# Attention scores in float32r parts on half the array's rows, with the operand stacks copied head by head inside SBUF

## The reference

```
attn = softmax(einsum('bgdi,bgdj->bgij', q, k) * 16**-0.5)     # 2 x 8 heads, each 1024 x 1024
x = x + proj(Wp, bp, einsum('bgij,bgdj->bgdi', attn, v))
```

## Time and profile before

| | us |
|---|---|
| median of 3 runs | 368.35 (367.45 to 369.86) |
| the profiled execution | 367.55 |
| its span, first to last instruction | 365.6 |
| PE busy | 309.8 (85%) |
| DVE busy | 258.9 (71%) |
| ACT busy | 194.1 (53%) |
| POOL busy | 103.9 (28%) |
| mean granted PE clock | 0.925 |

### The profile page before, as it was taken

How to read it: one execution, slowest core, us unless ns; L and a number is a source line. 1 busy time by engine, 2 the same in 40 slices (tenths; PEclk the granted TensorE clock), 3 DMA queues, 4 the chain that set the end, 5 groups by cost and what they waited for, 6 DMA issues and landing times.

```text
span 365.6 us, 5601 instructions
## 1 busy us (share of the span) xinstructions
PE 309.8 (85%) x2046; PEld 106.8 (29%) x2046; DVE 258.9 (71%) x270; ACT 194.1 (53%) x359; POOL 103.9 (28%) x137
## 2 busy tenths in 40 slices
PE   7568779999990599999989999998981999698796
PEld 2244123333320133333323333333220344222242
DVE  3746759898970177887748988879898146999820
ACT  1406347767760267767757666766760546453132
POOL 5000051111010011011000036999980100894410
PEclk9969699999995599999999999999995799969899
DMA  5168950000699300000000000590000001960001
GB/s 198 29 210 129 162 104 3 30 31 0 125 120 125 37 1 2 1 2 3 1 2 0 2 2 3 158 204 5 1 2 0 0 0 74 192 167 2 0 0 57
DMA packets 11022, 19.97 MB, mean 55 GB/s; under 512 B 2035, under 2 KB 2931, under 8 KB 10995
## 3 DMA queue, kind: packets, MB, share of 16 engines
q1 hardware_dynamic: 10998, 19.64, 26.6%
HBM read 13.61 MB, written 5.54 MB: 52 GB/s over the span
## 4 chain that ended last, share of the span: by engine, by line
PE 59%; DVE 20%; DMA 9%; issue 4%; SPq 3%; ACT 2%; POOL 2%; DVEq 0%; ACTq 0%; POOLq 0%
PE ps L971 15%; PE ps L930 15%; PE ps L960 12%; DVE qs L744 11%; DMA qs<-mrows 6%; PE ps L1122 4%; DVE mx L696 4%; DMA ks<-parts_dram 2%; PE ps L1136 2%; SPq L331 2%; PE ps L951 2%; PE ps L1081 2%; PE ps L876 2%; PE ps L902 1%; ACT pr L568 1%
## 5 line engine op out<-in xcount | busy, mean ns | idle before, releaser
L696 DVE TENSOR_REDUCE mx<-ps 128x1 f32<-128x1024 f32 x128 | 154.3, 1221 | 55.5 <-PE ps L930 51.0
L568 ACT ACTIVATE pr<-ps 128x512 f32<-128x512 f32 x256 | 139.0, 595 | 98.8 <-PE ps L960 98.7
L960 PE MATMUL ps<-qs,ks 99*128 99x512 bf16 x256 | 79.6, 389 | 17.8 <-DMA qs<-mrows 16.9
L930 PE MATMUL ps<-ks,qs 96*128 96x512 bf16 x256 | 79.4, 395 | 10.7 <-DMA ks<-part 5.5
L971 PE MATMUL ps<-pr,va 128*32 128x256 f32 x1024 | 83.5, 398 | 0.0
L744 DVE SCALAR_TENSOR_TENSOR qs<-xpad,w,qs 128x512 f32<-128x512 f32 (+1 forms) x35 | 54.7, 1562 | 1.0
L433 POOL TENSOR_TENSOR mparts<-zeros,mx 128x8 bf16<-128x8 f32 x16 | 3.7, 230 | 169.0 <-DVE mx L696 169.0
L960 PEld LDWEIGHTS ps<-qs,ks 99*128 99x128 bf16 x256 | 24.5, 99 | 61.2 <-DMA qs<-mrows 16.7
L971 PEld LDWEIGHTS ps<-pr,va 128*32 128x32 f32 x1024 | 20.3, 109 | 51.4 <-issue 46.8
L930 PEld LDWEIGHTS ps<-ks,qs 96*128 96x128 bf16 x256 | 17.0, 99 | 55.5 <-issue 44.2
L1056 PE MATMUL ps<-xr,wt 128*32 128x512 f32 x224 | 30.0, 664 | 3.5 <-DMA xr<-pad_dram 3.5
(11 more groups left out here) (99 smaller groups left out, 229.2 us busy)
## 6 DMA issues: line engine op xcount, KB each, us to landing
parts_dram<-part SPq DMA_DIRECT2D x12, 256.0 KB, 2.6
xr<-pad_dram SPq DMA_DIRECT2D x8, 361.0 KB, 6.2
qs<-parts_dram SPq DMA_DIRECT2D x6, 256.0 KB, 11.6
ks<-parts_dram SPq DMA_DIRECT2D x6, 256.0 KB, 15.8
xr<-pad_dram SPq DMA_DIRECT2D x4, 304.0 KB, 10.7
qs<-parts_dram SPq DMA_DIRECT2D x6, 192.0 KB, 4.9
ks<-parts_dram SPq DMA_DIRECT2D x6, 192.0 KB, 7.3
xr<-pad_dram SPq DMA_DIRECT2D x4, 285.0 KB, 10.3
```

The lines of the kernel that those rows point to most:

```text
L568: nc.scalar.activation(pr[:, j % PR, c * HALF:(c + 1) * HALF], st[c], ACT.Exp, scale=SCALE).then_inc(exp_done, 1)
L696: nc.vector.tensor_reduce(mx[:, r, i:i + 1], sm[i % 2], AX.X, ALU.max).then_inc(max_done, 1)
L930: last = nc.tensor.matmul(sm[i % 2][:, c * HALF:(c + 1) * HALF], qs[0:STACK, bass.ds(s * N + i * P, P)], ks[0:STACK, bass.ds(s * N + c * H ...
L960: nc.tensor.matmul(st[c], ks[0:ROWS, bass.ds(t * N + j * P, P)], qs[0:ROWS, bass.ds(t * N + c * HALF, HALF)], start=True, stop=True).then_ ...
```

## The change

Queries and keys become two float32r parts (`PARTS = 2`), three products of parts in 3 x 16 = 48 rows, and 50 rows with the maxima (now positive, against rows of -1 in `ks`). A stack lies in partitions 0 to 49 or 64 to 113 (`rows_of`), and `qs` and `ks` shrink to four slots: two groups of rows by two cells of columns (`cell_of`). Head t uses the slot of head t - 4. The plan runs almost two heads ahead (`LAG = 1`, 15 tiles first), so that tile and transposed scores mostly belong to different groups of rows, and PE's order in a step alternates a half of `scores_t` (one step further ahead than before) and a half of `scores`. The stacks are copied from `hl` inside SBUF, six DMAs a head: for heads 0 and 1 the queries by SP and the keys by ACT's queue, for the others all by SP. POOL's `split_max` has two operations in place of five. The convolution's sums move to `hl` of image 1, so DVE's and POOL's taps wait for the stack of head 15. `replicate(0)` comes after `row_max(12)`.

```
-PARTS = 3                                   +PARTS = 2
-STACK = 6 * D                               +TERMS = 3; STACK = TERMS * D; GROUP_ROWS = 64; CELLS = 2
-LAG = 3                                     +LAG = 1; GAP = 3
+def max_turn(t): return 3 if t <= FINISH else 6 if t == FINISH + 1 else 5
+def u_turn(t): return 5 if t <= FINISH else 3
+def rows_of(t): return t // 2 % 2 * GROUP_ROWS
+def cell_of(t): return t % 2 * N
+        def stack(queue, i, t, n):
+            order, dst = ((Q_ORDER, qs), (K_ORDER, ks))[i]
+            queue.wait_ge(S(f"part{i}{n}", t // HEADS), 1)
+            h = t % HEADS
+            for g in range(TERMS):
+                if order[g] == n:
+                    queue.dma_start(
+                        dst[rows_of(t) + g * D:rows_of(t) + (g + 1) * D, cell_of(t):cell_of(t) + N].bitcast(F32),
+                        hl[h * D:(h + 1) * D, t // HEADS, i, n, :].bitcast(F32)).then_inc(S("stack", t), 16)
...
+            def next_stack(t):
+                sp.wait_ge(st_ready, 2 * NT * (t - 3))
+                for n in range(PARTS):
+                    stack(sp, 0, t, n)
+                    stack(sp, 1, t, n)
...
+            row_max(0)
+            for t in range(1, T):
+                if t + 3 < T:
+                    next_stack(t + 3)
+                row_max(t)
+                if t == FINISH + 3:
+                    replicate(0)
...
+            def scores_t(n, c):
+                t, j = divmod(n, NT)
+                if n:
+                    t_.wait_ge(exp_done, 2 * n + c - 1)
+                if j == 0 and c == 0:
+                    t_.wait_ge(s_mrow[t % 2], 16 * (t // 2 + 1))
+                rows = slice(rows_of(t), rows_of(t) + ROWS)
+                nc.tensor.matmul(st[c], ks[rows, ...], qs[rows, ...], start=True, stop=True).then_inc(st_ready, 1)
...
+            (head t, step j of PE; n = 8t + j)
+                    if n + 1 < NT * T:
+                        scores_t(n + 1, 0)
+                    if here:
+                        scores(*here[0], 1)
+                    if n:
+                        times_v(n - 1)
+                    if n + 1 < NT * T:
+                        scores_t(n + 1, 1)
+                    if j == max_turn(t) and t + 1 < T:
+                        turn_max(t + 1)
+                    if j == u_turn(t) and t:
+                        turn_u(t - 1)
...
+                    if then:
+                        scores(*then[0], 0)
```

More of the change, by code:

```diff
@@ L28 @@
 BF16 = mybir.dt.bfloat16
+F32R = mybir.dt.float32r
 ACT = mybir.ActivationFunctionType
@@ L531, in _ @@
                 a.wait_ge(S(f"proj{i}", 0), 1)
[L532 to L535, removed]
+                nc.scalar.activation(hl[:, 0, i, 0, :], sm[i], ACT.Identity, bias=vec(V_BQ + i))\
+                    .then_inc(S(f"part{i}0", 0), 1)
+            for n in range(PARTS):
+                for t in range(2):
+                    stack(nc.scalar, 1, t, n)
             values(0)
@@ L556, in copy_u, with head @@
+            def copy_u(t):
                 a.wait_ge(pv_done, NT * t + NT)
-                if later(t, 2):
+                if t >= 2:
                     a.wait_ge(ot_ready, t - 1)
-                nc.scalar.activation(u[:, r, :], pv[:, 0:2 * P], ACT.Copy).then_inc(u_ready, 1)
-            def head(t, r, turn=LAG + 2, also={}):
+                nc.scalar.activation(u[:, t % 2, :], pv[:, 0:2 * P], ACT.Copy).then_inc(u_ready, 1)
+            def head(t, also={}):
                 for j in range(NT):
+                    n = NT * t + j
@@ L579, in copy_oc @@
                 nc.scalar.activation(oc[:, 0, :], sm[0], ACT.Copy).then_inc(S("oc", 0), 1)
-            copy_max(0, 0)
-            head(0, 0)
-            head(1, 1)
-            with a.Fori(1, FINISH // 2) as pair:
-                head(2 * pair, 0)
-                head(2 * pair + 1, 1)
-            for t in range(FINISH - 1, T - 2):
-                head(t, t % 2, turned(t), also={LAG: copy_oc} if t == FINISH else {})
+            copy_max(0)
+            for t in range(T - 2):
+                head(t, {LAG + 1: copy_oc} if t == FINISH else {})
             def ln_square(k):
@@ L682, in _ @@
             v.wait_ge(S("w_soon"), 16)
-            split_rest(0)
+            low_part(0)
             gn_vareps(v, 1)
-            split_rest(1)
-            for i in range(2):
-                split_low(0, i)
+            low_part(1)
             gn_apply(v, 1, xs[:, 1, :], xn[:, 1, :], S("xn", 1))
@@ L951, in turn_u @@
                     last = nc.tensor.transpose(mi[:, OT_AT + i * P:OT_AT + (i + 1) * P],
[L952 removed]
+                                               u[:, t % 2, i * P:(i + 1) * P], ident)
                 last.then_inc(ot_ready, 1)
[L955 to L962 removed]
@@ L1036, in _ @@
                     t_.wait_ge(S("copied1"), 1)
-                    turn_max(0, 0)
-            t_.wait_ge(S("kones"), 16)
+                    turn_max(0)
+            t_.wait_ge(S("kones"), 32)
             t_.wait_ge(S("va", 1), 1)
+            for c in range(2):
+                scores_t(0, c)
+            scores(*plan[0][0][0], 0)
             also = {FINISH: [(LAG, finish_turn), (LAG + 2, finish_project)],
```

422 lines of the change are left out of this document (177 added, 245 removed).

## The result

The changed kernel takes 548.63 us (median of four runs, 540.85 to 552.13), the kernel before in the same job 369.11 (367.45 to 370.97): ratio 1.473, 95% interval 1.454 to 1.493. The direction was predicted; the size was not: 409, in a range of 382 to 452. The profiled execution took 547.0 us, span 545.2, mean granted clock 0.640 where it was 0.925.

The account below looks back on a forecast made before the run. PE's own order bound a plain head (12.6 us), DVE after head 13. Head 0 ends at 53.3, twelve waits add 69.6, heads 1 to 11 129.8; first tap 40.6 us later, span 406.2, forecast 409 us, range 382 to 452.

Parts of the forecast that it names:

- The order of SP's queue: Maxima's DMA behind next_stack's wait and six copies on SP: PE empty 5.8 us, twelve times, 69.6 in all.
- Rivals 2 and 3: SP's queue: 2, wait only 1.9 us, 342 us, chance 0.07; 3, wait 4.6, no clock lost, 374 us, 0.07.
- Side by side, in one pass: PE's score and transposed-score halves: float32r in one pass, two row groups at once, 0.22 us a pair instead of 0.44.
- Rival 1: PE's score pairs not side by side, or float32r taking twice the passes: 40 us more, 449 us; chance 0.20.
- The clock: After each PE wait, 4.7 us at half clock: 1.7 us lost, twelve times and once at the start; ends 0 and 2.1.
- 10.1 us a head: Plain head bound by DVE: eight maxima of 1.15 us, a division of 0.56, 0.3 for imperfect order; instead of 12.6.
- Head 0's transposed scores: Start of head 0 on PE: predicted at 41.5 us, before 41.98, with stacks landing about 1.6 us earlier.
- The tail: From DVE's first convolution tap to the span's end: kept at 117.2 us.
- The replicas: Head 12: replicate(0) before row_max(13) holds the maxima's DMA 14.5 us; a head covers all but 2.7.

Follow-up runs that it names:

- the filled kernels: changed_64 and side_by_side_64, whose score matmuls take in zero rows up to 62 and 64; 488.12 and 399.53 us.
- changed_64: The changed kernel, SP's order and waits kept, with score matmuls filled with zero rows to 62 and 64; 488.12 us, ratio 1.323.
- one_row_group_128: The changed kernel with row_max(t) before next_stack(t + 3), all stacks in one row group, zero rows to 126 and 128; 397.74 us, ratio 1.077.
- before_with_waits: The kernel before, with the wait of next_stack and eight 64 KB copies ahead of row_max(1) to row_max(12); 462.18 us, ratio 1.252.
- side_by_side_64: The changed kernel with row_max(t) before next_stack(t + 3) and zero rows to 62 and 64, pairs side by side; 399.53 us, ratio 1.08.
- copy_max_later: side_by_side_64 with ACT's copy of the turned maxima moved one step back in heads 0 to 9; 388.63 us, ratio 1.045.
- before_48_rows: The kernel before with two bf16 parts and three products, so 48 and 51 rows instead of 96 and 99; 487.48 us.

## Why the prediction was right in sign and wrong in size

**The order of SP's queue: right.** Predicted twelve waits of 5.8 us, 69.6 in all; the trace has 69.4. Issues 3.72 (3.9), landing 2.11 (2.0). Rivals 2 and 3 are out. What decided was six issues in a row: one alone, 0.62, is under a third of that landing, so what the prediction set side by side, six issues and one landing, says nothing on single DMAs. With the lost clock it is 7.4 a head where I had 7.5, by the filled kernels. That nearness is partly luck: 70.3 us of waits leave 1.5 a head for the clock (I had 1.7), but in changed_64 the clock was away for 3.6 to 21.4 us after a wait and not for 4.7, and it slowed heads of 13.45 us, not of 10.1.

**Side by side, in one pass: right.** Both kinds start at 177.09 together. The Trainium skill, TensorEngine Tiling (Array Packing), § Tiling Modes, says that different tiles can work in parallel; the trace agrees. For a half's 0.22 us stands one_row_group_128, where at 2.4 GHz the halves follow each other and start 0.23 and 0.24 apart (151.00 and 151.23, 152.69 and 152.93). Rival 1 is out; the range's upper end of 452 came from it and so from the wrong doubt. One thing was missed: the prediction took all pairs as side by side, and those at every second head's change are not.

**The clock: wrong, and the largest error.** The step was "with 4.7 us at half clock ... 1.7 us, twelve times". I took the 4.7 from a kernel whose score matmuls drive 96 and 99 rows. With 48 and 50 the clock took 10.9 to 17.6 us to return after three of the twelve waits, and did not return before the next one after the others: from 64 to 433 us it was high for 24. 60.5 us go when zero rows fill the groups. With the matmuls of the kernel before it takes 3.6 to 7.4 us, as before_with_waits shows; a trace with one such wait could not tell even that. My ends for this term, 0 and 2.1, came from the same rows and so shared their condition. The whole run at 1.2 GHz was no end of mine: at the measured cold step of 2.16 us the 128 steps alone are 276 us.

**10.1 us a head: wrong.** DVE was to be the bound, "and 0.3 for imperfect order". At 2.4 GHz a head takes 13.45 (side_by_side_64) and DVE idles. The transposed scores now run one step ahead, in front of whatever ACT waits for, and wait for ACT's exponentials themselves; I costed each engine's work, and not the loop between two of them. The runs show 0.7 of the 3.35 us as such a loop (copy_max_later) and some 0.3 as pairs in one group; the rest is not shown. 3.35 us over 14 plain heads are 47 us, an estimate, since side_by_side_64 has eight such heads at full clock.

**The other terms.** Head 0's transposed scores start at 48.39, predicted 41.5, 6.9 us later: the first scores start at 21.30 as before (21.29) and not 1.6 earlier, and the clock is low for longer there too. The tail is 1.5 longer than its 117.2. Of the 139 us between predicted and measured span, 60.5 are the rows, 47 the longer heads, 8.4 these two; some 23 are not split up. changed_64, with a clock of 0.797, still has long stretches at 0.50: after its waits the clock was away 49 us longer in all than 12 x 4.7. At 2.16 us a step instead of 13.45 / 8 = 1.68 that is an estimated 11 us; the rest stays open.

**The replicas.** They went out at 374.82 and `row_max(13)` was issued at 394.46 without a long wait at its turn: a head at half clock covers them. That step cost nothing where I had 2.7.

## What to carry to other kernels

A cheaper matmul is not only fewer rows: in all five kernels here in which the score matmuls drove 48 to 67 rows without zero rows (three one after the other, two side by side) and nothing filled PE's gaps, TensorE lost 2.4 GHz for long stretches. Zero rows up to 96 and 99 or 126 and 128 gave it back (0.951, 0.953), zero rows up to 62 and 64 side by side only in part (0.797, 0.865), and no matmul got longer by them: with 126 and 128 rows a half takes 0.23 to 0.24 us, with 96 and 99 it took 0.22. When a change alters what TensorE's instructions look like, the time at which the clock returned in the old trace is no bound; take the whole run at 1.2 GHz as one end. And where a change issues one engine's work further ahead, cost the round trips between the engines in that order, not just each engine's sum.

## What the hardware showed that I had not expected

- Zero rows decide the clock: 32 of them are 458.77 against 352.97 us. What exactly the chip counts stays open. It is not the data's content, since zeros do as well; nor only the rows driven at one moment, since under twelve waits 48 and 50 side by side have 0.640 and 96 or 99 in one matmul 0.848.
- At 1.2 GHz PE looks fully busy (30.00 of 30.00 us in before_48_rows). Busy time alone would have called it a bound; the clock column shows that it is a symptom.
- Side by side and one after the other gave the same time once the rows were filled: 399.53 and 397.74 us. The first has shorter heads at full clock (13.45 against 15.39 us), the second keeps its clock better (0.953 against 0.865).
